# Row 0's attention maxima formed inside the mixer's last step, row 1's in its tail

## The reference

```python
x = _layernorm(x + _L0_attn_ref(x, W_in, conv_w, conv_b, A_log, D_param, dt_bias, W_out))   # the mixer
x = _layernorm(x + _L0_xattn_ref(x, ctx_512, ctx_512))
x = _layernorm(x + _L0_ffn_ref(x, gate, expert_bias, w1, w2, w3, shared_w1, shared_w2, shared_w3))

# the mixer: project x, convolve val, then per head a decaying, causal product
val, gate, Bp, Cp, dt = split(x @ W_in.T)
M = einsum('blhn,bmhn->bhlm', C, B) * exp(masked differences of the cumulated decay)
Y = (M @ val + carried state + D * val) * silu(gate);  out = Y @ W_out.T

# attention, 32 query heads on 8 key heads of width 8
scores = einsum('bkgsd,bktd->bkgst', qh, kh) / sqrt(8)
out = einsum('bkgst,bktd->bkgsd', softmax(scores), vh)
```

## Time and profile before

| | |
|---|---|
| Median of 3 runs | 750.16 us (749.89 to 752.26) |
| The profiled execution, its own time | 750.16 us |
| Its span in the trace | 748.1 us |
| TensorE busy | 720.6 us, 96% |
| VectorE | 569.4 us, 76% |
| ScalarE | 441.3 us, 59% |
| GpSimd | 382.4 us, 51% |
| Granted TensorE clock, mean | 0.994 |

### The profile page before, as it was taken

The page is one execution under the profiler, slowest core; times in us unless marked ns, Lnnn a source line. Parts: engine busy times, 40 slices in busy tenths (PEclk is TensorE's granted clock), DMA queues, the critical chain, the costliest instruction groups (busy, mean ns, idle before and its releaser), DMA issues. The chain is left out here.

```text
span 748.1 us, 17083 instructions
## 1 busy us (share of the span) xinstructions
PE 720.6 (96%) x5874; PEld 397.9 (53%) x5874; DVE 569.4 (76%) x1102; ACT 441.3 (59%) x869; POOL 382.4 (51%) x423
## 2 busy tenths in 40 slices
PE   8799999999999999999999999999979999989897
PEld 3456555555655556565555656565633333335464
DVE  5677858687685868768586877978788999886877
ACT  7844446654444665444466554464647777867576
POOL 2877527463352746335274963656310431369644
PEclk9999999999999999999999999999999999999999
DMA  6575312326622232652213342422004200000001
GB/s 209 181 223 187 70 57 56 74 44 102 179 64 56 57 76 46 106 174 61 56 56 80 77 101 71 83 58 57 1 16 142 97 16 23 24 0 2 29 31 56
DMA packets 34297, 57.90 MB, mean 77 GB/s; under 512 B 7056, under 2 KB 11920, under 8 KB 33680
## 3 DMA queue, kind: packets, MB, share of 16 engines
q1 hardware_dynamic: 33680, 57.08, 29.7%
q10 hardware_dynamic: 576, 0.31, 0.1%
HBM read 54.10 MB, written 2.36 MB: 75 GB/s over the span
## 5 line engine op out<-in xcount | busy, mean ns | idle before, releaser
L292 POOL TENSOR_TENSOR cum_rows<-cum_rows,cum_t 128x512 f32<-128x512 f32 x128 | 136.7, 1078 | 194.1 <-DMA cum_rows<-cum_scratch 194.1
L808 PE MATMUL pring<-xt_hi,w_hi 128*128 (+1 forms) x576 | 171.8, 380 | 0.0
L808 PE MATMUL pring<-xt_hi,w_lo 128*128 (+1 forms) x576 | 171.5, 379 | 0.0
L808 PE MATMUL pring<-xt_lo,w_hi 128*128 (+1 forms) x576 | 171.5, 379 | 0.0
L660 DVE TENSOR_TENSOR bt<-pring,bt 128x512 f16<-128x512 f32 x128 | 88.1, 688 | 72.1 <-ACT bt L449 72.0
L449 ACT CAST bt<-pring 128x512 f16<-128x512 f32 x128 | 74.5, 582 | 111.5 <-PE pring L808 111.3
L664 DVE TENSOR_TENSOR ct<-pring,ct 128x512 f16<-128x512 f32 x128 | 88.2, 689 | 53.9 <-ACT ct L453 53.5
L850 PEld LDWEIGHTS pscore<-ct,bt 128*128 128x128 f16 x1536 | 96.0, 98 | 34.7 <-issue 6.8
L850 PE MATMUL pscore<-ct,bt 128*128 128x128 f16 x1536 | 106.7, 219 | 3.9 <-DVE mt L632 2.0
L453 ACT CAST ct<-pring 128x512 f16<-128x512 f32 x128 | 74.7, 584 | 52.6 <-PE pring L808 52.6
L808 PEld LDWEIGHTS pring<-xt_hi,w_lo 128*128 128x128 f16 x576 | 56.3, 98 | 68.0
(11 more groups left out here) (166 smaller groups left out, 961.6 us busy)
## 6 DMA issues: line engine op xcount, KB each, us to landing
cum_rows<-cum_scratch SPq DMA_DIRECT2D x32, 1024.0 KB, 8.0
w_raw<-in_w_in SPq DMA_DIRECT2D x35, 256.0 KB, 6.2
q_rows<-in_xt SPq DMA_DIRECT2D x4, 512.0 KB, 10.5
acc<-in_x SPq DMA_DIRECT2D x1, 2048.0 KB, 7.6
vals<-in_vals SPq DMA_DIRECT2D x16, 128.0 KB, 2.1
out<-acc SPq DMA_DIRECT2D x7, 256.0 KB, 2.2
w_raw_e<-in_w_up SPq DMA_DIRECT2D x1, 1024.0 KB, 5.5
w_raw_e<-in_w_gate SPq DMA_DIRECT2D x1, 1024.0 KB, 4.8
```

The costliest lines, as they stand in the source:

```text
L292: nc.gpsimd.tensor_tensor(rows[:, par, :, q], rows[:, par, :, q], own, ALU.subtract).then_inc(sem("since"), 1)
L808: mm = nc.tensor.matmul(bank[name][:], w[:, c, k, cols], x[:, k, bass.ds(n % TB, 1), :].rearrange("p o n -> p (o n)"), start=(i == 0), sto ...
```

## The change

The eight maxima of row 0 move from the tail into slots 3 to 7 of the last mixer step. Each is one matmul ahead of a B or C projection, into a score bank that is free at that moment (`max_places`, `max_bank`), and one reduction ahead of the low half of that projection. A score group now also waits until the maximum in its bank is reduced (`maxima_read`). For this VectorE's last step is taken out of its loop and written out.

The maxima of row 1 take the place of row 0's in the tail, with the same banks and the same order. The transpose of row 0's maxima stands at the tail's start, in `pring1`, its negation is ScalarE's next operation, and the last output projection, which writes that bank, waits for the negation. Row 1's transpose and negation stand where row 0's were. SyncE still copies row 0's negated maxima in the mixer's block; row 1's are copied by the first instruction of attention's block.

Attention's head has no maxima of row 1 any more, and alternates shifted scores of row 0 with maxima of row 2.

```diff
+        late_max = [pring[2], pring[3], pscore[1]]
+        mx_t = [pring[1][0:32, 0:L], pring[2][0:32, 0:L]]
+        max_places = [(3, "B"), (3, "C"), (4, "B"), (4, "C"), (5, "B"), (6, "B"), (6, "C"), (7, "B")]
+        def max_bank(i):
+            s, k = max_places[i]
+            return pscore[(s + (k == "C")) % 2]
+        def maxima_at(s, k):
+            return [i for i, place in enumerate(max_places) if place == (s, k)]
...
 # ScalarE, behind the last step
+            def negate_max(b):
+                act.wait_ge(sem("mx_turn"), b + 1)
+                nc.scalar.mul(neg_mx[:, b], mx_t[b], -1.0).then_inc(sem("neg_max"), 1)
+            negate_max(0)
             evac_q(8)
...
-            act.wait_ge(sem("mx_turn"), 1)
-            nc.scalar.mul(neg_mx[:, 0], mx_t, -1.0).then_inc(sem("neg_max"), 1)
+            negate_max(1)
...
 # VectorE, the step
+            def first_row_max(i):
+                dve.wait_ge(sem("max_mm"), i + 1)
+                nc.vector.tensor_reduce(mx[:, 0, :, i], max_bank(i)[:].rearrange("p (k n) -> p k n", k=4), AX.X, ALU.max).then_inc(sem("max_red"), 1)
...
+                for s in range(3, SLOTS):
+                    if maxima:
+                        for i in maxima_at(s, "B"):
+                            first_row_max(i)
                     low_b(n, s)
+                    if maxima:
+                        for i in maxima_at(s, "C"):
+                            first_row_max(i)
                     low_c(n, s)
                     weigh(n, s - 1)
+                    if s == 3:
+                        pad_values(n)
+                        continue
                     if norm:
...
-            with dve.Fori(STEPS - TB + 1, STEPS) as n:
+            with dve.Fori(STEPS - TB + 1, STEPS - 1) as n:
                 step(n, norm=True)
+            step(STEPS - 1, norm=True, maxima=True)
...
 # TensorE, the step
+            def maxima_read(pe, bank_, below):
+                last = max([i for i in range(below) if max_bank(i) is bank_], default=-1)
+                if last >= 0:
+                    pe.wait_ge(sem("max_red"), last + 1)
+            def first_row_scores(n, i):
+                s, k = max_places[i]
+                pe.wait_ge(sem("mixed"), 8 * n + s + (3 if k == "B" else 4))
+                if i == 0:
+                    pe.wait_ge(sem("k_load"), 16 * 28)
+                maxima_read(pe, max_bank(i), i)
+                nc.tensor.matmul(max_bank(i)[:], q_rows[:, 0, i // 4, i % 4, :], k_rows[:, 0, i // 4].rearrange("p k n -> p (k n)"),
+                                 start=True, stop=True).then_inc(sem("max_mm"), 1)
...
-                    pair(n, s)
+                    for k, half in (("B", 0), ("C", 1)):
+                        for i in maxima_at(s, k) if maxima else ():
+                            first_row_scores(n, i)
+                        project(n, f"{k}{s}", s + 1, half, ("b_proj", "c_proj")[half])
+                    if maxima:
+                        maxima_read(pe, pscore[s % 2], len([p for p in max_places if p[0] <= s]))
                     scores(n, s - 1)
...
 # TensorE, the tail
             scores(STEPS, -1)
-            pe.wait_ge(sem("k_load"), 16 * 28)
+            pe.wait_ge(sem("c_evac"), 8 * STEPS + 1)
+            turn_max(0)
...
+            pe.wait_ge(sem("neg_max"), 1)
             out_project(STEPS, last=True)
...
-            pe.wait_ge(sem("max_red"), 8)
-            nc.tensor.transpose(mx_t, mx[:, 0].rearrange("p k i -> p (k i)"), ident[:]).then_inc(sem("mx_turn"), 1)
+            turn_max(1)
...
 # attention: SyncE
+            store_max(1, 1)
             load_values(0, 0)
             load_values(1, 1)
-            store_max(1, 1)
...
 # attention: ScalarE
-            negate_max(1, 1)
...
 # attention: VectorE
-            for i in range(8):
-                row_max(1, 1, i, early=True)
...
 # attention: TensorE
-            for i in range(4):
-                for_max(1, i, early=True)
-            for i in range(3):
-                shifted(0, 0, i)
-            for i in range(4, 8):
-                for_max(1, i, early=True)
-                if i < 7:
-                    shifted(0, 0, i - 1)
+            for what in "D0 D1 F0 F1 F2 D2 F3 D3 F4 D4 F5 D5 F6 D6 F7 D7".split():
+                (shifted(0, 0, int(what[1])) if what[0] == "F" else for_max(2, int(what[1])))
             times_values(0, 0, 0)
-            shifted(0, 0, 6)
-            shifted(0, 0, 7)
-            for_max(2, 0)
-            for_max(2, 1)
-            turn_max(1, 1)
-            for i in range(2, 8):
-                for_max(2, i)
```

More of the change, by code:

```diff
@@ L737, in first_step, with step @@
                 dve.wait_ge(sem("cw_half"), 3)
-            def step(n, norm=False):
+            def first_row_max(i):
+                dve.wait_ge(sem("max_mm"), i + 1)
+                nc.vector.tensor_reduce(mx[:, 0, :, i], max_bank(i)[:].rearrange("p (k n) -> p k n", k=4), AX.X, ALU.max).then_inc(sem("max_red"), 1)
+            def step(n, norm=False, maxima=False):
                 convolve(n, 0)
@@ L926, in turn_q, with step @@
                 mm.then_inc(sem("q_turn_mm"), 1)
-            def step(n, queries=()):
+            def maxima_read(pe, bank_, below):
[10 more added lines that the diff above has]
+                                 start=True, stop=True).then_inc(sem("max_mm"), 1)
+            def step(n, queries=(), maxima=False):
                 project(n, "val", 0, 0, "val_proj")
@@ L954, in _, with turn_max @@
             step(STEPS - 2, range(0, 4))
-            step(STEPS - 1, range(4, 8))
+            step(STEPS - 1, range(4, 8), maxima=True)
+            def turn_max(b):
+                pe.wait_ge(sem("max_red"), 8 * b + 8)
+                nc.tensor.transpose(mx_t[b], mx[:, b].rearrange("p k i -> p (k i)"), ident[:]).then_inc(sem("mx_turn"), 1)
             def for_max(i):
@@ L963, in for_max @@
                 else:
[L964 to L967, removed]
+                    pe.wait_ge(sem("max_red"), 8 + i - 2)
+                q = q_rows[:, 1:2, i // 4, i % 4, :].rearrange("p o n -> p (o n)")
+                k = k_rows[:, 1:2, i // 4].rearrange("p o k n -> p (o k n)")
+                nc.tensor.matmul(late_max[i % 3][:], q, k, start=True, stop=True).then_inc(sem("max_mm"), 1)
             scores(STEPS, -1)
-            pe.wait_ge(sem("k_load"), 16 * 28)
+            pe.wait_ge(sem("c_evac"), 8 * STEPS + 1)
+            turn_max(0)
             for i in range(3):
@@ L1017, in attention_and_experts @@
         pmx_t = pmax[max_turns.index("turn") % 3][0:32, 0:L]
-        early_max = pmax + [pturn]
         def max_bank(i):
@@ L1588, in for_max @@
                 k = k_rows[:, bass.ds(b, 1), t].rearrange("p o k n -> p (o k n)")
[L1589 to L1592, removed]
+                max_free(b, i)
                 if i == 0 and b >= late:
                     pe.wait_ge(sem("q_rows"), b - late + 1)
-                scores = early_max[i % 4] if early else max_bank(i)
-                nc.tensor.matmul(scores[:], q, k, start=True, stop=True).then_inc(sem("max_mm"), 1)
+                nc.tensor.matmul(max_bank(i)[:], q, k, start=True, stop=True).then_inc(sem("max_mm"), 1)
             def shifted(b, slot, i):
```

18 lines of the change are left out of this document (5 added, 13 removed).

## The result

| | before | changed |
|---|---|---|
| Median of 7 runs | 751.73 us (748.95 to 753.22) | 745.91 us (744.99 to 747.87) |
| Ratio of the runs | | 0.9943, 95% interval 0.9926 to 0.9960 |
| The profiled execution, its own time | 750.16 us | 745.75 us |
| Its span | 748.1 us | 743.7 us |
| TensorE busy | 720.6 us | 717.8 us |

The ratio is an estimate over all runs, not the quotient of the two medians, which is 0.9923. The kernel became faster as the sum said, and by somewhat more.

A forecast was written before the change was run, and what follows sets the result against it. TensorE was taken to bound the kernel nearly throughout, VectorE the tail and attention's head. The terms +1.73 + 0.69 - 1.0 - 4.45 gave -3.0 us on 750.16: forecast 747.2 us, range 745.7 to 749.2.

The forecast's parts named there:

- Eight matmuls, +1.73: Mixer's last step: eight added matmuls each cost a full TensorE their start-to-start time of 0.216 us, +1.73 us.
- The stall ahead of score group 4, +0.69: Last step, slot 5: TensorE waits for reduction 4, queued behind VectorE's statistics, +0.69 us; no other slot stalls.
- The tail unchanged: Mixer's tail: row 1's reductions replace row 0's, so it moves as a block; extra transpose and negation hidden, uncovered some 0.5.
- The block's end, -1.0: Between the blocks: SyncE's transfer no longer drains last, VectorE does; 1.0 us gained, bounds 0 and 1.1.
- The head, -4.45: Attention's head: transpose of row 2's maxima 7.01 us after the first matmul instead of 11.46, with seven matmuls at half clock.
- The forecast's least gain of 0.5 us: Attention's head: lower bound of its gain, if the clock stays down to the transpose of row 2's maxima.
- its own 10.8: Attention's head, rival at 3%: clock stays down to the transpose, which comes at 10.8 instead of 7.0 us; 751.0 us total.
- The clock that stays up: Between the blocks, rival at 12%: shorter idle stretch keeps full clock, transpose at 5.83 us instead of 7.01; 746.0 us total.
- Normalising pair slow: Last step, slot 7, rival at 13%: the pair takes 2.12 us, stalling score group 6 by 0.96; up to +1.9, 749.1 us.
- block's end nothing: Between the blocks, rival at 7%: the earlier end of SyncE's transfer gains nothing; 748.2 us total.
- VectorE the bound: Last step, rival at 8%: VectorE becomes its bound, five score groups each wait 1.3 us; +2.8 us, 753.0 us total.

The follow-up runs named there:

- experiment 5: The changed kernel with each of the eight matmuls of row 0's maxima issued twice into the same bank: 749.32 us, ratio 0.9981.
- Experiment 4: The changed kernel with row 0's reduction 4 moved ahead of the normalisation's statistics on VectorE: 747.01 us, ratio 0.9954.
- Experiment 2: The kernel before, with SyncE's transfer of row 0's negated maxima moved to be attention's first instruction: 750.13 us, ratio 1.000.
- experiment 1: The changed kernel with row 1's transfer put back at the end of the mixer's block: 748.22 us, ratio 0.9974.
- experiment 9: The changed kernel run again with nothing altered, on the same chip as a further version: 746.76 us, ratio 0.9945.
- experiment 6: The changed kernel with each of row 0's eight reductions done twice, the first into a spare tile: 747.61 us, ratio 0.9951.
- experiment 8: The kernel before, with eight useless matmuls behind the transpose of row 0's maxima to keep TensorE busy: 749.34 us, ratio 0.9988.
- experiment 7: The changed kernel with row 1's transfer back at the mixer block's end, plus eight useless matmuls behind TensorE's last transpose there: 747.07 us, ratio 0.9958.
- experiment 3: The changed kernel's last step with row 0's maxima, no maxima in the tail, attention's head as in the kernel before: 750.43 us, ratio 0.9996.
- experiment 10: The changed kernel with reduction 4 ahead of the statistics, ten maxima in the last step, six in the tail, last query turn earlier: 744.65 us; another chip 744.05.

## Why the prediction was right, and where its size was off

- **Eight matmuls, +1.73.** Right: experiment 5 found the price by doubling them.
- **The stall ahead of score group 4, +0.69.** Right in place, cause and total. The record shows a wait of 0.50 us, but what counts is the delay: slot 5's outputs come 1.75 later, less five matmuls of 0.216 that is 0.67. The last three matmuls bring it to 2.40 by the tail's outputs (forecast 2.42). Experiment 4 takes 0.67 away by that one reduction's place. The slots that the forecast gave room had it.
- **The tail unchanged.** Right: from its outputs to attention's first matmul it took 9.95 us before and 8.96 now, and the difference is the block's end; the transpose, the negation and the wait for it show nowhere.
- **The block's end, -1.0.** Right: -0.99. Experiment 2 gives the same 0.99 to the kernel before, experiment 1 takes 0.87 back.
- **The head, -4.45.** The mis-sized term: -5.39 in the profiled execution, -3.97 in a second profile of the same kernel (experiment 9). The step that failed is the one that took the half clock of the earlier trace rows over for seven matmuls of the new head. Those at the start were a fact of one execution of the kernel before, whose clock had fallen 0.4 us ahead of the first matmul. In the changed kernel there were none, or, in experiment 9, a stretch at half clock of about the same length that began 1.3 us behind the first matmul, so that all of it fell on matmuls. The clock was one of two outcomes and not a value in between: the forecast's 7.01 lies between 6.07 and 7.49 and was met by neither. For a full clock the forecast's own rival had 5.83 us; 6.07 was measured. The reasoning on queues held to 0.24 us, half of which came ahead of the last maximum: it started at 3.68 instead of 3.55, behind shifted scores that wait for ScalarE's exponentials. (The forecast's least gain of 0.5 us does not follow from its own 10.8, which leaves 0.7.)
- **Weights of the rivals.** The clock that stays up had 12%. Of the six profiles with a 1.33 us stretch (the changed kernel twice, experiments 2, 4, 5, 6) five kept it, as did those with 1.16 to 1.60; the two with 2.2 to 2.3 us lost it. The evidence at hand, a stretch cut from 2.32 to 1.33, deserved more; that the length of the stretch decides is not shown, since only two profiles have the long one. The Trainium skill (TensorE: Matmul & The Clock Gate, "What's actually happening") says that activity is sampled in periods that do not line up with the kernel, so the same kernel can meet the change at another place. The traces agree: the same instructions took 6.07 and 7.49 us, and the clock fell 0.4 us ahead of the head's first matmul in the kernel before and 1.3 to 1.4 us behind it in experiments 9 and 1.
- **Normalising pair slow, block's end nothing, VectorE the bound.** None occurred: 0.73 us, 0.99 us, and experiment 6.

That the measured change came out larger than forecast in the profiled executions is in part luck: the one profile of the kernel before met the low clock in its head, and the first profile of the changed kernel did not. With the clock alike in both the traces give 2.6 us (low in both) or 2.8 (full in both), near the forecast's 3.0.

What stays open is the rest between the traces and the medians. A ratio of 0.9943 on 750 us is 4.3 us, with an interval from 3.0 to 5.6 us, which holds the traces' 4.0 (low clock before, full clock after) and not the 2.6 or 2.8. How often either kernel's head meets the low clock in the executions without a trace was not measured, and the medians also hold spells of the low clock elsewhere (last section).

## What to carry to other kernels

Work moved from a stretch where one engine sets the pace to one where that engine waits pays the difference of both: here 1.7 us of a full TensorE and a queue stall of 0.7 bought 4.2 us of a head that VectorE led (10.30 against 6.08 us, experiments 8 and 7, both at full clock). It pays only if the freed place is used: row 0 alone brought attention's first matmul 0.40 us later. The 1.0 us of the block's end can be had without moving any work (experiment 2). Write out both queues around each new wait, since the one stall came from an unrelated pair of statistics ahead of a reduction and went away by swapping them. Look at which engine ends last before a block ends: here a DMA issued as SyncE's last instruction held up every engine for 0.87 to 0.99 us, and the same transfer could be the next block's first, where its reader came 1.9 us or more behind its issue.

## What the runs showed that was not expected

- The clock can fall after work has resumed: some 1.3 us behind the first matmul of the head in experiment 9, with TensorE fully busy, and it stayed at 0.50 for some three microseconds. A 0.50 in a window need not have the idle stretch right ahead of it.
- Executions differ by a spell of the low clock far from the change. The last step's first outputs came at 508.4 to 510.1 us in eight profiles and at 511.4 to 514.2 in five, and in those five the windows of 20 us show a clock below 1.00 early in the mixer (0.91 in 20 to 40 us, in one of them again in 40 to 60), where the other eight have 1.00. The shift is 3 us and more, as much as the whole change. It shows without traces too: over the 81 executions of the kernel before that ran beside the experiments, a mean granted clock lower by 0.001 goes with 0.7 to 0.8 us more. Medians at unlike clocks can't be compared to half a microsecond; places inside a trace can.
- The length of a drain is no cost of its own. VectorE's took 1.71 us in the kernel before and in the changed one and 0.70 in experiments 3 and 10, but in all of them it ended within 0.1 us of the end of VectorE's last addition (550.31 and 550.3 before, 552.23 and 552.3 changed). What counts is where the last operation of the last engine ends; in experiment 3 that was ScalarE's copy.
